# Row maxima of one group found in two halves, and ScalarE's copies moved among its exponentials

## The reference

```python
xn = (x - moving_mean) * rsqrt(moving_var + 0.001) * gamma + beta
q = xn @ Wq + bq ; k = xn @ Wk + bk ; v = xn @ Wv + bv
scores = einsum('bhid,bhjd->bhij', q, k) * 64 ** -0.5
attn = softmax(scores, axis=-1)
out = einsum('bhij,bhjd->bhid', attn, v) @ Wo + bo
return xn + out
```

## Time and profile before

| | |
|---|---|
| median of 3 runs | 4872.09 us (4872.04 to 4872.81) |
| the profiled execution's own time | 4878.3 us |
| its span in the profile | 4876.3 us |
| busy share PE / DVE / ACT / POOL | 99% / 90% / 89% / 93% |
| granted TensorE clock | 1.00 of full speed |
| moved by DMA | 806 MB, 165 GB/s |

### The profile page before, as it was taken

One profiled execution on the slowest core, in us unless ns is written; L12 is line 12 of the kernel. 1 busy time (PEld: TensorE's weight loads), 2 busy tenths in 40 slices (PEclk: granted clock), 3 DMA queues, 4 the chain that ended last, 5 costly groups with the idle time before them and its releaser, 6 DMA issues.

```text
span 4876.3 us, 170133 instructions
## 1 busy us (share of the span) xinstructions
PE 4840.4 (99%) x51224; PEld 4029.0 (83%) x51224; DVE 4403.0 (90%) x6946; ACT 4332.4 (89%) x18949; POOL 4511.3 (93%) x2824
## 2 busy tenths in 40 slices
PE   7999999999999999999999999999999999999999
PEld 5888888888888888888888888888888888888887
DVE  6999999999999999999999999999999999999998
ACT  6888888888888889888888888888889888888887
POOL 6999999999999999999999999999999999999997
PEclk9999999999999999999999999999999999999999
DMA  7888888888888888888888888888888888888886
GB/s 132 168 168 166 168 165 168 167 166 166 167 167 167 167 167 166 168 168 166 168 166 168 166 166 167 167 167 167 167 167 166 168 168 167 168 166 168 166 166 136
DMA packets 4294233, 806.24 MB, mean 165 GB/s; under 512 B 4294208, under 2 KB 4294208, under 8 KB 4294208
## 3 DMA queue, kind: packets, MB, share of 16 engines
q1 hardware_dynamic: 4293312, 805.80, 83.9%
q10 hardware_dynamic: 896, 0.13, 0.0%
HBM read 537.10 MB, written 268.44 MB: 165 GB/s over the span
## 4 chain that ended last, share of the span: by engine, by line
PE 99%; DVE 0%; ACT 0%; issue 0%; DMA 0%; SPq 0%; DVEq 0%
PE probsT_ps L634 21%; PE score_ps L601 21%; PE uo_ps L618 20%; PE uo_ps L654 19%; PE g_ps L644 18%; ACT probs L329 0%; DMA bias_col<-in_L_conv_bv 0%; ACT g L356 0%; ACT probsT L344 0%; PE uo_ps L582 0%; SPq L191 0%; DVE row_stat L479 0%; DVE probsT L526 0%; DVE y L465 0%; DVE xT L536 0%
## 5 line engine op out<-in xcount | busy, mean ns | idle before, releaser
L329 ACT ACTIVATE probs<-score_ps,neg_top 128x128 f32<-128x128 f32 x8192 | 2916.2, 385 | 479.6 <-DVE neg_top L489 479.6
L271 POOL TENSOR_TENSOR x_weighted<-x_in,row_weights 128x1024 f32<-128x1024 f32 x1024 | 2401.7, 2368 | 21.9 <-DVE x_weighted L432 21.9
L329 ACT ACTIVATION_READ_ACCUMULATOR probs<-score_ps,neg_top 128x1 f32 x8192 | 1836.2, 224 | 0.0
L479 DVE TENSOR_REDUCE row_stat<-score_ps 128x8 f32<-128x1024 f32 x1024 | 1250.4, 1221 | 221.8 <-PE score_ps L601 197.6
L293 POOL TENSOR_TENSOR y<-attn,x_scaled_rows 128x512 f32<-128x512 f32 x768 | 979.8, 1276 | 338.6 <-DVE attn L445 338.6
L634 PE MATMUL probsT_ps<-ident,probs 128*128 128x128 f32 x8192 | 1272.1, 278 | 5.3 <-ACT probsT L344 4.0
L654 PEld LDWEIGHTS uo_ps<-w_o,uT 128*128 128x128 f32 x8192 | 1075.0, 191 | 243.3 <-issue 242.8
L634 PEld LDWEIGHTS probsT_ps<-ident,probs 128*128 128x128 f32 x8192 | 925.1, 141 | 413.2 <-issue 364.5
L282 POOL TENSOR_TENSOR x_scaled_rows<-x_weighted,out_bias 128x512 f32<-128x512 f32 x1024 | 1197.3, 1193 | 0.0
L654 PE MATMUL uo_ps<-w_o,uT 128*128 128x128 f32 x8192 | 1164.4, 275 | 0.0
L644 PE MATMUL g_ps<-xT,w_g 128*128 128x512 f32 x2048 | 1053.9, 596 | 8.2 <-ACT g L356 4.7
(11 more groups left out here) (68 smaller groups left out, 1381.2 us busy)
## 6 DMA issues: line engine op xcount, KB each, us to landing
x_quads<-in_x SPq DMA_DIRECT2D x4096, 64.0 KB, 2.2
x_in<-in_x SPq DMA_DIRECT2D x1024, 256.0 KB, 3.4
out<-y SPq DMA_DIRECT2D x1024, 256.0 KB, 2.4
norm_row<-in_L_conv_gamma ACTq DMA_DIRECT2D x1, 32.0 KB, 2.7
norm_row<-in_L_conv_beta ACTq DMA_DIRECT2D x1, 32.0 KB, 3.6
norm_row<-in_L_conv_bo SPq DMA_DIRECT2D x1, 32.0 KB, 3.1
norm_row<-in_L_conv_moving_mean ACTq DMA_DIRECT2D x1, 32.0 KB, 3.2
norm_row<-in_L_conv_moving_var ACTq DMA_DIRECT2D x1, 32.0 KB, 4.0
```

Source lines behind the costliest of these rows:

```text
L271: nc.gpsimd.tensor_tensor(x_weighted[:, n % 4, :, 0:2 * C].rearrange("p s (h c) -> p s h c", h=2), x_in[:, n % 8, :, None, :].broadcast_to ...
L329: last = nc.scalar.activation(probs[:, n % 4, q, :], score_ps[n % 2][:, q // PAIRS, q % PAIRS * W:(q % PAIRS + 1) * W], ACT.Exp, bias=neg_ ...
L479: nc.vector.tensor_reduce(row_stat[:, s, :, NEG_MAX].rearrange("p (h k) -> p h k", h=2), score_ps[n % 2][:].rearrange("p h (k w) -> p h k ...
```

## The change

DVE finds the maximum and the shift of the even group of each step (2t) in two halves, one for each of its two PSUM banks, with semaphores of their own; the odd group is as before. ACT waits for these semaphores. On ACT, the copies of transposes and the copy of g stand behind other numbers of exponentials: the first copy of transposes behind 7 exponentials of the even group where it stood behind 5, the g copy behind all 8 where it stood behind 6, the second copy behind 5 of the odd group where it stood behind 4.

```diff
@@ ACT
             def exponentials(r, n, peeled, rows):
                 if not exists(r, n, peeled):
                     return
                 s = parts(n)
+                if HALF in rows and n % 2 == 0:
+                    act.wait_ge(neg_top_b_found[s], uses(r, n))
                 if 0 in rows:
-                    act.wait_ge(neg_top_found[s], uses(r, n))
+                    act.wait_ge((neg_top_a_found if n % 2 == 0 else neg_top_found)[s], uses(r, n))
                     if exists(r, n - 4, peeled):
@@
             def step(r, t, peeled):
-                exponentials(r, 2 * t, peeled, range(0, 5))
+                exponentials(r, 2 * t, peeled, range(0, 7))
                 keep_probsT(r, 2 * t - 2, peeled, 0)
-                exponentials(r, 2 * t, peeled, range(5, 6))
+                exponentials(r, 2 * t, peeled, range(7, 8))
                 keep_g(r, 2 * t + 4, peeled)
-                exponentials(r, 2 * t, peeled, range(6, 8))
-                exponentials(r, 2 * t + 1, peeled, range(0, 4))
+                exponentials(r, 2 * t + 1, peeled, range(0, 5))
                 keep_probsT(r, 2 * t - 1, peeled, 0)
-                exponentials(r, 2 * t + 1, peeled, range(4, 8))
+                exponentials(r, 2 * t + 1, peeled, range(5, 8))
                 keep_probsT(r, 2 * t - 1, peeled, 1)
                 keep_g(r, 2 * t + 5, peeled)
@@ DVE
+            def find_max_half(r, n, peeled, h):
+                if not exists(r, n, peeled):
+                    return
+                s = parts(n)
+                if h == 0:
+                    dve.wait_ge(scores_made[s], uses(r, n))
+                nc.vector.tensor_reduce(row_stat[:, s, h * HALF:(h + 1) * HALF, NEG_MAX],
+                                        score_ps[n % 2][:, h, :].rearrange("p (k w) -> p k w", k=PAIRS),
+                                        AX_X, ALU.max, negate=True).then_inc((max_a_found if h == 0 else max_b_found)[s], 1)
+
+            def find_shift_half(r, n, peeled, h):
+                if not exists(r, n, peeled):
+                    return
+                s = parts(n)
+                dve.wait_ge((max_a_found if h == 0 else max_b_found)[s], uses(r, n))
+                if h == 0:
+                    dve.wait_ge(neg_const_found[parts(n | 1)], uses(r, n | 1))
+                nc.vector.tensor_reduce(neg_top[:, s, h * HALF:(h + 1) * HALF],
+                                        row_stat[:, s, h * HALF:(h + 1) * HALF, NEG_MAX:ROW_CONST + 1], AX_X,
+                                        ALU.add).then_inc((neg_top_a_found if h == 0 else neg_top_b_found)[s], 1)
@@ DVE step
-                find_max(r, 2 * t, peeled)
-                find_shift(r, 2 * t, peeled)
+                for h in range(2):
+                    find_max_half(r, 2 * t, peeled, h)
+                    find_shift_half(r, 2 * t, peeled, h)
                 find_max(r, 2 * t + 1, peeled)
```

More of the change, by code:

```diff
@@ L108, in build @@
         max_found = sem_ring("max_found")
+        max_a_found = sem_ring("max_a_found")
+        max_b_found = sem_ring("max_b_found")
         neg_const_found = sem_ring("neg_const_found")
         neg_top_found = sem_ring("neg_top_found")
+        neg_top_a_found = sem_ring("neg_top_a_found")
+        neg_top_b_found = sem_ring("neg_top_b_found")
         const_found = sem_ring("const_found")
```

## The result

The changed kernel takes 5206.01 us (median of 4 runs, 5204.25 to 5206.54) against 4872.07 before: a ratio of 1.0684, 95% interval 1.0666 to 1.0703. It is slower by 334 us. The profiled span is 5204.5.

A forecast was written before the change was run, and what follows sets the result against it. PE was taken to bound the kernel, busy 99%, with ACT already holding it by 0.09 a step. Next scores at 10.03 against 9.41 give 0.62 over about 511 steps, 317 us: 4872 + 317 = 5189, within 5082 to 5260.

The forecast's parts named there:

- The two waits ahead of the first exponential: On ACT, all seven exponentials of group 2t wait for both halves' shifts; ACT idle about 1.6 us a step before them.
- The first rival: On ACT, the first exponential goes ahead after the first half, at 2.13; period 9.32, time 4826 us; chance 0.04.
- DVE's chain: On DVE, maximum and shift in halves take 1.72 in place of 1.47; first exponential 0.24 later, at 2.92.
- The first copy, and PE's second transposes: ACT's copy behind seven exponentials starts at 5.34, not 4.57; PE's second transposes at 6.10, not 5.46: a 0.64 stall.
- The g copy: On ACT, g behind eight exponentials starts at 6.21; PE's second projection at 7.05 where PE gets there at 6.98: 0.07 more.
- the term that decides: The late first copy on ACT, which stalls PE's second transposes of group 2t-2 by 0.64 a step.
- PE behind it: On PE, after the second projection at 7.05, transposes 0.86 later and next scores at 10.03, not 9.41: 0.62 a step.
- The high bound: First exponential at 3.00, PE restart costing 0.12 more, second projection 7.19, next scores 10.17: +0.76 a step, 5260 us.
- The clock: TensorE's granted clock stays 1.00; the rival, PE pauses bringing 2.4 to 1.2 GHz, gives over 9000 us; chance 0.01.

The follow-up runs named there:

- The run with three ahead: The kernel before, with the second copy of transposes (group 2t-1) behind 3 exponentials of the odd group and not 4: 4881.42 us, ratio 1.0021.

## Why the prediction was right

The forecast was 5189, in a range of 5082 to 5260; measured 5206. Its steps:

- **The two waits ahead of the first exponential**: right. ACT's idle time ends with the second shift (1.65 to 1.66 a step, forecast 1.6), and moving the one line takes away 395 us. The first rival, 4826, was wrong for this kernel, and its time was near for the one with the wait moved (4811).
- **DVE's chain**: from the first half maximum to the first exponential 1.72 was forecast and is 1.72 (2011.14 to 2012.86); a half maximum 0.69, measured 0.687. By the Trainium skill's table in "VectorE: DVE Perf Modes" (TRN2 errata) it would be (120 + 512) / 0.96 GHz, 0.658 us, and the half shift 0.073, where the trace has 0.17. The measured ones decide: the line through two durations of this kernel was the better price. The same section says below its table that the fixed term of a copy was measured at about 150 cycles; an estimate with it, (150 + 512) / 0.96 GHz, is 0.690, and the trace agrees with that one.
- **The first copy, and PE's second transposes**: copy at 5.34, as forecast; transposes at 6.12, forecast 6.10. PE's idle time 257.5 us, forecast 245.
- **The g copy**: the second projection at 7.04 (2006.91 less 1999.87, the start of that step's scores one period of 10.06 earlier), forecast 7.05. I called the copy of transposes the term that decides, with 0.07 added by g. That is the working of one order of events and a poor reading of cause: the run with the copy early shows that g alone holds PE as long.
- **PE behind it**: the period is 10.06, forecast 10.03. The step that was short is the one from the second projection to the next transposes, taken as 0.86: it is 0.93 (2006.91 to 2007.84) and the two records take 1.10 and not 1.02. The same 1.10 stands wherever this projection starts just behind ACT's g copy, in the run with g late too. With g early, it is 1.02 again. Against these 0.07 stand 0.03 from the last transposes to the scores, which take 0.53 and not 0.56. So two misses cancel in part, and that the sum came out so near owes something to luck. In all 0.65 a step and not 0.62: 511 steps make 332, of 334 measured. Between the two profiles, whose spans are 328 apart, PE's idle time grew by 255 us and its busy time by 74: the transposes start 0.66 late, and only 0.50 of that shows as idle, since the modelled ends hide the rest.
- **The high bound**: it took 0.12 for a restart of PE from two figures that are not alike, 0.56 to the next scores and 0.44 to the next outputs. To the scores it is 0.56 after a wait and 0.53 without, so 0.03. The range held without it.
- **The clock**: in the steady part 1.00 from 2000 to 3000 us, as forecast. The argument for it was misread: the 0.97 of the first 50 us is a mean, and a fall is hidden in it (below).

## What to carry to other kernels

A wait that a helper issues ahead of its loop holds every instruction of the call: when a dependency is split, look at which call the second wait lands in, and put it at the first instruction that needs it. Work split for an earlier start pays only together with an order that uses it; here the early start alone gave nothing, the new order alone lost 203 us, and both together, with the second wait in its right place, gave 1.2%. Where an engine is 99% busy, lay one step out by start times and work out the margin of each hand-over. In the kernel before one held PE by 0.09 a step, and three more had little to spare: the first copy of transposes 0.15 us, the first g copy 0.07, and the bank of scores that ACT's last exponential reads 0.16. The run with three ahead mended the one and used up the last.

## What was not expected of the hardware

The granted clock of TensorE fell in the fill, twice in the changed kernel and once in the kernel before. Stretches: engines' busy us, granted clock, DMA share, GB/s. First the changed kernel, then the kernel before.

```profile
42.00:47.00 5.00, 3.48 (x16) 2.01 (x18) 1.76 (x3) 4.74 (x24) 5.00 (x4) 0.66 0.19 31
...
53.00:61.00 8.00, 7.06 (x46) 5.36 (x48) 3.41 (x7) 4.58 (x20) 0.00 (x0) 0.57 0.00 0
```
```profile
42.00:46.00 4.00, 3.78 (x20) 2.40 (x22) 1.30 (x3) 4.00 (x22) 4.00 (x4) 0.57 0.19 32
```

The second fall of the changed kernel lies behind a pause of 2.62 us, and the scores that follow take 3.53 where they take 2.06 in the steady part. The fall in the kernel before lies behind a pause of 1.80:

```profile
52.24 0.63 PE L661 MATMUL probsT_ps<-ident,probs 128*128 128x128 f32 x4 [2.62 <-ACT probsT L350]
...
57.37 3.53 PE L628 MATMUL score_ps<-xT,g 64*128 64x128 f32 x32
```
```profile
42.22 1.75 PE L644 MATMUL g_ps<-xT,w_g 128*128 128x512 f32 x2 [1.80 <-ACT g L356]
43.90 3.07 PE L601 MATMUL score_ps<-xT,g 64*128 64x128 f32 x32
```

So I was wrong that the rows speak against such a fall: there was one in the first 50 us of the kernel before itself. The Trainium skill ("TensorE: Matmul & The Clock Gate", on the clock gate) says that an idle engine falls to the lower clock, and has cases here, for a few us each. These rows don't show that a pause alone decides: in the run with the first copy late and g early PE pauses for 3.01 us in the fill, and the clock stays at 1.00 from 40 to 70 us.

```profile
42.63 1.10 PE L671 MATMUL g_ps<-xT,w_g 128*128 128x512 f32 x2 [3.01 <-ACT g L362]
```

The pauses of 0.50 in every later step left the clock at 1.00: it is 1.00 from 100 to 2000, from 2000 to 3000 and from 3000 to 4700 us.
